# Another order of the steady turn's calls on four engines of a fused attention and expert layer

## The reference

```
h = layernorm(x) * (1 + ca) + sa
x = x + ga * attention(h)     # rms norm, 16 heads of 64, causal softmax, sigmoid gate per head, output projection
h = layernorm(x) * (1 + cb) + sb
x = x + gb * (mlp(h) + experts(h))
```

## Time and profile before

| What | Value |
| --- | --- |
| median of 3 runs | 1451.83 us |
| the profiled execution's own time | 1448.72 us |
| its span | 1446.8 us |
| TensorE busy | 1395.7 us (96%) |
| VectorE busy | 1288.8 us (89%) |
| ScalarE busy | 1270.4 us (88%) |
| GpSimd busy | 1054.2 us (73%) |
| chain that ended last | TensorE 81%, ScalarE 14% |
| granted TensorE clock | 9 of 10 or more in all 40 slices |
| steady turns | windows 655.0 to 698.5 and 698.5 to 742.0: TensorE busy 42.79 and 42.80 of 43.50 us |

### The profile page before, as it was taken

How to read it: one execution, slowest core, us unless ns; L and a number is a source line. 1 busy time by engine, 2 the same in 40 slices (tenths; PEclk the granted TensorE clock), 3 DMA queues, 4 the chain that set the end, 5 groups by cost and what they waited for, 6 DMA issues and landing times.

```text
span 1446.8 us, 39838 instructions
## 1 busy us (share of the span) xinstructions
PE 1395.7 (96%) x11491; PEld 1159.5 (80%) x11491; DVE 1288.8 (89%) x5345; ACT 1270.4 (88%) x4212; POOL 1054.2 (73%) x1221
## 2 busy tenths in 40 slices
PE   6899999999999999999999999999999999999988
PEld 4678878888878888878888878888878888878878
DVE  6689999999999999999999999999999999999977
ACT  6799988898988898988898988898988898988884
POOL 2057878787878787878787878787878787878760
PEclk9999999999999999999999999999999999999999
DMA  4000000000000000000000000000000000000000
GB/s 132 16 18 18 18 7 20 20 20 16 15 9 20 20 20 16 15 9 20 20 20 16 15 9 20 20 20 16 15 9 20 20 20 16 15 9 24 14 11 10
DMA packets 51041, 27.74 MB, mean 19 GB/s; under 512 B 10336, under 2 KB 50208, under 8 KB 51008
## 3 DMA queue, kind: packets, MB, share of 16 engines
q1 hardware_dynamic: 50768, 26.91, 7.2%
q10 hardware_dynamic: 240, 0.43, 0.1%
HBM read 23.02 MB, written 4.31 MB: 19 GB/s over the span
## 4 chain that ended last, share of the span: by engine, by line
PE 81%; ACT 14%; issue 2%; DVE 1%; DMA 0%; SPq 0%; POOL 0%; ACTq 0%; DVEq 0%; POOLq 0%
PE pW L1457 10%; PE pS L1527 9%; PE pW L1540 9%; PE pW L1568 8%; PE pW L1459 8%; PE pW L1458 8%; PE pS L1517 7%; PE pS L1513 6%; PE pW L1610 4%; PE pW L1613 4%; ACT pS L660 4%; ACT pT L652 4%; PE pW L1544 3%; PE pW L1601 2%; ACT qk L642 2%
## 5 line engine op out<-in xcount | busy, mean ns | idle before, releaser
L660 ACT ACTIVATE pS<-pS,nmx 128x128 f32<-128x128 f32 (+1 forms) x1024 | 389.4, 433 | 32.9 <-DVE nmx L1085 32.9
L504 POOL TENSOR_TENSOR fexp<-fexp,fsum 128x512 f32<-128x512 f32 x240 | 299.9, 1284 | 76.4 <-DVE fexp L1214 76.4
L1085 DVE CUSTOM_DVE_ANT_0 pS<-pS,mask 128x128 f32<-128x128 f32 (+1 forms) x1024 | 331.3, 387 | 23.2 <-PE pS L1517 18.6
L652 ACT COPY pT<-pS 128x768 f32<-128x768 f32 x256 | 216.2, 845 | 39.6 <-PE pS L1527 37.7
L495 POOL TENSOR_TENSOR fsum<-ex 128x512 f32<-128x512 f32 x248 | 250.8, 1054 | 0.0
L1527 PE MATMUL pS<-ident,p_sb 128*128 128x128 f32 x1536 | 215.0, 276 | 6.1 <-DVE p_sb L1105 4.1
L1105 DVE TENSOR_TENSOR p_sb<-pS,coef 128x256 f32<-128x256 f32 (+2 forms) x512 | 210.2, 452 | 8.9
L1527 PEld LDWEIGHTS pS<-ident,p_sb 128*128 128x128 f32 x1536 | 172.7, 140 | 36.6 <-issue 17.3
L660 ACT ACTIVATION_READ_ACCUMULATOR pS<-pS,nmx 128x1 f32 x1024 | 193.9, 189 | 0.0
L642 ACT COPY qk<-pW 128x512 f32<-128x512 f32 x256 | 162.1, 633 | 4.1 <-PE pW L1459 0.6
L1540 PE MATMUL pW<-pT,v 128*64 128x256 f32 x1024 | 165.4, 401 | 0.3 <-ACT pT L652 0.2
(11 more groups left out here) (211 smaller groups left out, 3694.7 us busy)
## 6 DMA issues: line engine op xcount, KB each, us to landing
x_in<-in_L_attn_tokens SPq DMA_DIRECT2D x32, 128.0 KB, 2.1
x_res<-in_L_attn_tokens SPq DMA_DIRECT2D x32, 128.0 KB, 3.0
modB<-mods_dram SPq DMA_DIRECT2D x32, 128.0 KB, 2.9
modA<-mods_dram SPq DMA_DIRECT2D x31, 128.0 KB, 3.1
out<-yo SPq DMA_DIRECT2D x31, 128.0 KB, 1.9
modC<-mods_dram SPq DMA_DIRECT2D x32, 64.0 KB, 3.1
fsum<-in_L_attn_Wkv SPq DMA_DIRECT2D x1, 512.0 KB, 6.1
w_out<-in_L_attn_Wout SPq DMA_DIRECT2D x1, 512.0 KB, 7.2
```

The costliest lines, as they stand in the source:

```text
L504: ins = nc.gpsimd.tensor_tensor(fexp[:, k, h, :], fexp[:, k, h, :], fsum[:, k, h].rearrange("p i j -> p (i j)"), ALU.mult)
L652: nc.scalar.copy(pT[:, p % 2], pS[:, p % 2, :, 0:SW]).then_inc(S(pT_ready), 1)
L660: ins = nc.scalar.activation(ps, ps, ACT.Exp, bias=nmx[:, p % 2, h, k:k + 1], scale=-1.0, accum_out=den(p)[:, h, k:k + 1])
L1085: ins = nc.vector.tensor_tensor_reduce(out=ps, in0=ps, in1=mask[:, (1 - k) * P:2 * P], scale=-1.0, scalar=LARGEST, op0=ALU.add, op1=ALU.mi ...
```

## The change

Calls change places in the lists of the steady turn on GpSimd, ScalarE, VectorE and TensorE. No instruction is added, removed or altered. The list `order`, and with it the order in which TensorE takes the four banks, stays as it is. The whole diff:

```
--- before.py
+++ after.py
@@ -590,10 +590,10 @@
                 weigh(0)
                 add_bias()
                 add_heads(0)
+                rstd1()
                 fold(0)
                 rstd2()
                 weigh(1)
-                rstd1()
                 add_heads(1)
                 rms1()
                 fold(1)
@@ -870,33 +870,33 @@
 
 
                 copy_transposes(7, -1)
+                values(0)
                 queries(2)
-                values(0)
                 queries(3)
+                values(3)
                 exp_scores(0)
                 weighted(6)
-                values(3)
                 gate_up(1)
                 exp_scores(1)
                 weighted(7)
                 down_tanh(0)
                 scale_head(1)
                 copy_transposes(0, 0)
-                down_tanh(1)
+                values(1)
                 copy_transposes(1, 0)
                 gate_up(2)
-                values(1)
+                down_tanh(1)
                 exp_scores(2)
+                exp_scores(3)
                 total(0)
                 weighted(0)
-                exp_scores(3)
-                copy_transposes(2, 0)
                 weighted(1)
                 queries(4)
+                gate_up(3)
                 scale_head(3)
+                copy_transposes(2, 0)
+                queries(5)
                 rows2()
-                gate_up(3)
-                queries(5)
                 copy_transposes(3, 0)
                 values(4)
                 modulate_h()
@@ -907,25 +907,25 @@
                 values(2)
                 exp_scores(5)
                 queries(7)
+                weighted(3)
                 values(5)
                 scale_head(5)
-                weighted(3)
                 copy_transposes(4, 0)
+                total(1)
                 copy_transposes(5, 0)
-                total(1)
+                experts(0)
                 weighted(4)
                 expert_exp(0)
                 rms_scale()
-                experts(0)
                 expert_exp(1)
                 high_part(xT_high, xT, "xT")
-                weighted(5)
                 experts(1)
                 exp_scores(6)
+                weighted(5)
                 exp_scores(7)
                 gate_up(0)
+                copy_transposes(6, 0)
                 queries(0)
-                copy_transposes(6, 0)
                 scale_head(7)
                 queries(1)
 
@@ -1377,16 +1377,16 @@
                 normalise(1)
                 gated_down(0)
                 choose(1, 0)
-                gated_down(1)
                 row_max(2)
                 row_max(3)
                 bias_product(2)
+                ln1_stats()
+                gated_down(1)
+                gate_product(2)
+                ln2_stats()
                 normalise(2)
-                ln2_stats()
-                gate_product(2)
+                normalise(3)
                 choose(1, 1)
-                normalise(3)
-                ln1_stats()
                 bias_product(3)
                 gate_product(3)
                 row_max(4)
@@ -1402,8 +1402,8 @@
                 low_part(xT_high, xT, "xT")
                 normalise(6)
                 finish()
+                normalise(7)
                 bias_product(0)
-                normalise(7)
                 gate_product(0)
                 if first:
                     split_rest()
@@ -1805,12 +1805,12 @@
                 project_out()
                 weigh_values(0)
                 weigh_values(1)
-                transpose_scores(2, 0)
                 project_qk(4)
                 gate_up(3)
+                transpose_scores(2, 0)
                 project_qk(5)
+                transpose_scores(3, 0)
                 project_v(4)
-                transpose_scores(3, 0)
                 scores(4)
                 transpose_h()
                 scores(5)
@@ -1823,19 +1823,19 @@
                 weigh_values(3)
                 transpose_scores(4, 0)
                 similarity(1)
+                transpose_experts(0)
                 transpose_scores(5, 0)
-                transpose_experts(0)
                 weigh_values(4)
+                scores(6)
                 weigh_values(5)
-                scores(6)
                 scores(7)
                 transpose_x()
                 transpose_experts(1)
                 project_ffn(0)
                 project_ffn(1)
                 gate_up(0)
+                transpose_scores(6, 0)
                 project_qk(0)
-                transpose_scores(6, 0)
                 project_qk(1)
 
             run(pe, body)
```

## The result

The changed kernel takes 1461.73 us (median of 6 runs, 1459.54 to 1465.80); the kernel before took 1452.44 us in the same measurement. The ratio is 1.0073, 95% interval 1.0063 to 1.0084: slower by 0.6 to 0.8%. The forecast was 1472, so the way was right and the rise was under half of the one forecast (+9.3 against +20 us). The time lies just inside the forecast's own range of 1461 to 1480.

What follows compares the result with a forecast made beforehand. TensorE was taken as the bound, with about 0.9 us a turn in reach. +0.44 us at scores(5) and +0.2 at the end made +0.65 x 31 = +20 us on 1451.83: 1472 us, range 1461 to 1480.

Steps and rivals of the forecast that it cites:

- step 4: VectorE/GpSimd port: earlier add_heads(0) blocks choose(1, 0), adding 0.9 us; 0.8 passed on, +0.44 us at scores(5).
- step 1: TensorE's middle: the 0.37 us stall at project_qk(4) goes, a new 0.37 us stall comes at transpose_scores(2).
- step 2: Changes between kinds of matmul on TensorE: about +0.2 us a turn in the middle and +0.2 at the end.
- step 3: Stretch up to scores(5): ScalarE's copy holds it at 683.6, so only 0.1 of the 0.54 us stall comes back.
- the case without the port: Rival in which choose(1, 0) stays ahead of add_heads(0): +3 us, 1455 us, chance 0.25.
- parts 1 to 3: TensorE's middle, changes of kind and stretch to scores(5) together: +0.1 us a turn, +3 us over 31 turns.
- step 5: Moves with cover on ScalarE, VectorE and GpSimd, such as values(0), rstd1, choose(1, 1), weighted(3): costed at 0.
- The port order does not turn: Rival: choose(1, 0) still goes ahead of add_heads(0) at the port; +3 us, 1455 us, chance 0.25.
- Faster: stalls go and changes of kind are free: Rival: TensorE's old stalls go, matmul kind changes hide in remaining stalls; -0.35 us a turn, 1441 us, chance 0.22.

Runs made afterwards that it cites:

- experiment 1: Changed kernel with normalise(7) put back behind bias_product(0) on VectorE: 1445.65 us, ratio 0.9965 to the kernel before.
- experiment 2: Kernel before with only normalise(7) moved ahead of bias_product(0) on VectorE: 1471.11 us, ratio 1.0135.
- experiment 3: Kernel before with normalise(7) ahead of bias_product(0) and choose(1, 0) moved behind row_max(3) on VectorE: 1450.70 us, ratio 1.0003.
- experiment 5: Changed kernel with choose(1, 0) moved behind row_max(3) on VectorE and ln1_stats in its old place: 1445.32 us, ratio 0.9960.
- experiment 7: Changed kernel with choose(1, 0) late, ln1_stats in its old place and TensorE's pairs weigh_values(4), weigh_values(5), scores(6), scores(7) whole again: 1452.41 us, ratio 1.0016.
- experiment 9: Changed kernel with whole pairs, a new middle on TensorE, ScalarE and VectorE, and the old end of the turn on TensorE and ScalarE: 1433.83 us, ratio 0.9888.
- experiment 6: Kernel before with only TensorE's pairs split into weigh_values(4), scores(6), weigh_values(5), scores(7): 1455.78 us, ratio 1.0036.
- experiment 8: Changed kernel with whole pairs and a new middle: transpose_scores(2) ahead of project_qk(4), ScalarE and VectorE reordered: 1444.29 us, ratio 0.9954.

## Why the prediction was right, and where its sizes were off

**The port (step 4) was the cause, and its size was right.** I had put `add_heads(0)` at 669.36 and `choose(1, 0)` at 669.42. In the trace after they are 0.03 us apart in the same order, and `choose(1, 0)` costs 0.86 us more (forecast 0.9). That the order would turn was a close call, at 0.06 us by my reckoning, and the chance of 0.46 said so. Experiments 1, 2, 3 and 5 show the cause from both sides: the edit that shifts GpSimd alone brings the loss, taking it back or taking `choose(1, 0)` out of the additions takes the loss away, with and without the rest of the change.

The block at L1214 is shown in the rows, and so is the order: the four instructions end by turns, GpSimd at 679.43, VectorE at 679.71, GpSimd at 680.84, VectorE at 681.13. That it is a lock over the whole instruction is what the Trainium skill says, page "SBUF — State Buffer", section "SBUF: two separate sides". The trace agrees, with 1.52 and 1.49 us for instructions of 0.54 beside additions of 1.27 and 1.45; the records of the two engines overlap by 0.1 to 0.3 us at each change, if each keeps the time that it takes alone, so where inside an instruction the lock is taken and given back is not shown.

**What VectorE passes on (steps 1 and 4): the mis-sized term.** The forecast +0.65 us a turn was +0.44 at `scores(5)` and +0.2 at the end. Measured are +0.14 (7.13 against 6.99), +0.18 (2.45 against 2.27) and some 0.06 elsewhere: +0.38. So the excess lies at `scores(5)`, and 0.27 of its 0.30 us is the stall ahead of `transpose_scores(2)`: 0.89 us, where the reckoning had 680.2 - 679.04 = 1.16. It is VectorE's stretch from `row_max(2)` to `ln2_stats`: I had 4.7 to 4.8 us, it is 4.52 (681.05 to 685.57), since durations overlap by more than the 0.1 that I took off. That leaves VectorE 0.3 us of slack ahead of `ln2_stats` and not 0.1. Of the port's 0.86 us so 0.55 reach `transpose_scores(2)` (3.20 us after `weigh_values(1)` against 2.65 in experiment 1), where I passed on 0.8. Without the port the new wait is 0.34 us (forecast 0.37).

**The changes of kind (step 2).** The end's +0.2 is +0.18 in the changed kernel and is paid. In the middle, from `weigh_values(1)` to `scores(4)` without the stalls, it is 5.90 - 0.89 = 5.01 us against 5.24 - 0.37 = 4.87: +0.14, where I had +0.2 and used +0.14 in step 3. What I missed is the use of the split: without it, the changed order of ScalarE would have made TensorE wait 0.44 us there (experiment 7).

**The stall ahead of `scores(5)` (step 3).** I let ScalarE's copy hold it at 683.6, a gain of 0.1 us. Experiment 1 has a gain of 0.30: the copy starts as reckoned (5.72 us after `weigh_values(1)`, forecast 5.77), but `scores(5)` follows its start at 0.97 and not at 1.08. In the changed kernel the copy holds nothing (0.37 us behind `transpose_h`), so this error is not in the forecast sum; it is in the case without the port, where parts 1 to 3 are worth -0.16 us a turn and not +0.1. Experiments 1 and 5, which are that case, came out 0.3 us a turn below what I expected.

The copy of experiment 1, with `scores(5)` at 682.90:

```profile
681.93 0.82 ACT L652 COPY pT<-pS 128x768 f32<-128x768 f32 x1
```

**The moves at 0 (step 5)** hold for the steady turn within the 0.06 us above, not for the turn of batch 1. That one went from 41.35 to 43.53 us, as large as six steady turns' loss. `weighted(5)`, behind `exp_scores(6)` now, frees the bank that `gate_up(0)` fills. In a steady turn the products of batch i-2 (`project_ffn`) lie between; in turn 1 there are none. TensorE after, in turn 1:

```profile
93.14 0.39 PE L1457 MATMUL pW<-h2T_high,s_g_high 128*128 128x256 f32 x1 [2.24 <-ACT aoT L642]
```

It stood 2.24 us (0.74 before, and 0.74 again in experiment 9, which has `weighted(5)` back in its old place). Experiment 1 has the same wait in its turn 1:

```profile
91.70 0.39 PE L1457 MATMUL pW<-h2T_high,s_g_high 128*128 128x256 f32 x1 [2.23 <-ACT aoT L642]
```

And the busy time of the engines in the 5 us behind it, after and then in experiment 1 (us, PE, PEld, DVE, ACT, POOL busy, granted clock, DMA share, GB/s):

```profile
93.00:98.00 5.00, 4.66 (x25) 4.46 (x26) 4.06 (x20) 4.34 (x15) 5.00 (x6) 0.68 0.07 16
```

```profile
91.50:96.50 5.00, 4.60 (x36) 3.92 (x37) 3.74 (x19) 4.71 (x16) 5.00 (x6) 1.00 0.10 28
```

After, the granted clock was 0.68 on average, part of it at the lower of its two levels; in experiment 1 it was 1.00, and turn 1 took 41.99 us. So of the 2.2 us the change accounts for 0.6 at full clock and the clock of that execution for 1.5. What lowered the clock is not shown: the same gap came with and without it. I had read only steady turns for the parts costed at nothing.

**The sum over the kernel.** The forecast took +0.65 for 31 turns. The 29 steady distances of +0.38 make 11.0 us, turn 1 adds 0.6 (2.2 with its clock), and the last distance gives back 0.3. The two profiled executions differ by 14.4 us, since the one after also came 1.6 us later to its first output projection. That start is where runs of one kernel scatter: in the eleven profiles it takes 66.2 to 70.3 us, with a mean granted clock of 1.00 down to 0.93, and from the second output projection to the last the clock is 1.00 in all of them. The medians differ by 9.3 us, less than the 11 to 13 of the turns. Three of the six runs after had a mean clock of 0.998 and took 1459.5 to 1460.4 us, the other three one of 0.994 to 0.995 and took 1463.1 to 1465.8; the clocks of the six runs of the kernel before are not on record, so how much of the difference is this scatter stays open.

**The rivals.** "The port order does not turn" fell with the row of 2.93 us. "Faster: stalls go and changes of kind are free" was half right: the old stalls are worth more than I gave them, but not because changes of kind are free. Experiment 1 is what the change would have been with the port order kept: faster by 0.35%. My 1455 us for that case was 9 us too high and on the wrong side of no change.

## What to carry to other kernels

Two engines that share a port are coupled without a semaphore: a call moved into an idle gap started another engine 0.33 us sooner and cost 1.35% (experiment 2). Before moving a call, list what the shifted engines run at the same moment, and put instructions that can block each other where the other engine waits anyway. And price an edit together with its partner: the split pairs cost 0.15 us a turn in one order and saved 0.14 in the other.

## What the runs showed of the hardware that was not expected

- A blocked pair doesn't cost one instruction but the pair: two instructions of 0.54 us take 2.07 us if VectorE starts 0.33 us ahead of GpSimd's additions, 2.93 to 2.96 if they start together, and 1.00 with none beside them. The two engines take turns: the instructions end alternately in the records.
- The cost is a step and not in proportion. Over all turns of the five profiles in which the two meet (before, after, experiments 1, 2 and 6), `choose(1, 0)` takes 1.97 to 2.21 us where VectorE's record starts 0.21 to 0.47 us ahead, and 2.92 to 2.99 where it starts together with the additions or up to 0.05 behind. The one turn with 0.11 us ahead took 3.08: to start first in the records by a little is not enough. The step is worth 0.5 to 0.7 us in a turn of 43.
- A gap of 2.24 us on TensorE was followed by a granted clock of 0.68 over 5 us in the changed kernel; one of 2.23 us at the same place in experiment 1 and one of 2.46 in experiment 8 left it at 1.00. The length of the gap alone does not settle it.
